# Graph layers on one core: GpSimd waits twice in a group of edges, and VectorE adds the edge bias

## The reference

```python
# layer 0
e = edge_attr @ W_edge + b_edge                 # 200000 x 128 by 128 x 256
msg = relu(x[src] + e)
agg = segment_sum(msg, dst)
h = relu(((1.0 + eps) * x + agg) @ W1 + b1) @ W2 + b2
x = layernorm(x + relu(batchnorm(h)))
# layer 1
z = x @ W                                       # 4 heads of 64
e = leaky_relu(es[src] + ed[dst]);  alpha = softmax of e over the edges of a dst
out = segment_sum(alpha * z[src], dst)
x = layernorm(x + out)
```

## Time and profile before

| | us |
|---|---|
| time before, median of 3 runs | 5048.78 (5046.24 to 5053.94) |
| the profiled execution's own time | 5007.87 |
| its span, first to last instruction | 5006.0 |
| PE busy | 3165.6 (63%) |
| POOL busy | 3022.7 (60%) |
| DVE busy | 2238.0 (45%) |
| ACT busy | 789.5 (16%) |

### The profile page before, as it was taken

How to read it: one execution, slowest core, us unless ns; L and a number is a source line. 1 busy time by engine, 2 the same in 40 slices (tenths; PEclk the granted TensorE clock), 3 DMA queues, 4 the chain that set the end, 5 groups by cost and what they waited for, 6 DMA issues and landing times.

```text
span 5006.0 us, 53159 instructions
## 1 busy us (share of the span) xinstructions
PE 3165.6 (63%) x13596; PEld 2405.9 (48%) x13597; DVE 2238.0 (45%) x4481; ACT 789.5 (16%) x1498; POOL 3022.7 (60%) x3229
## 2 busy tenths in 40 slices
PE   6878777887878778777864444444444444444455
PEld 4666655565656555555643333333333333333343
DVE  4333333333333323223355555555555555555566
ACT  2212111211222112112230000010101111111111
POOL 6666656666666556556456666666666666666654
PEclk9898888888888888888887777777777777776677
DMA  4444444444444434334254444444444444444443
GB/s 150 131 132 134 133 124 130 134 127 127 132 130 132 123 122 128 115 120 126 87 157 133 134 135 135 132 133 135 132 134 133 137 128 136 133 132 134 134 131 101
DMA packets 321267, 650.03 MB, mean 130 GB/s; under 512 B 149823, under 2 KB 170537, under 8 KB 321225
## 3 DMA queue, kind: packets, MB, share of 16 engines
q0 software_dynamic: 150272, 413.00, 29.0%
q1 hardware_dynamic: 164681, 230.37, 14.4%
q10 hardware_dynamic: 6272, 6.19, 0.4%
HBM read 636.22 MB, written 13.08 MB: 130 GB/s over the span
## 4 chain that ended last, share of the span: by engine, by line
another core or an unknown queue 36%; PE 20%; issue 19%; DVEq 12%; DVE 9%; ACT 2%; DMA 1%; SPq 0%; POOLq 0%; ACTq 0%
PE psum L1018 7%; PE psum L1029 5%; DVEq L1172 3%; PE psum L681 3%; DVEq L878 2%; DVEq L836 2%; DVE hot_t L869 2%; PE psum L1015 2%; DVE rows L1156 2%; DVEq L874 1%; DVEq L1167 1%; PE psum L1057 1%; DVE acc L1170 1%; PE psum L1038 1%
## 5 line engine op out<-in xcount | busy, mean ns | idle before, releaser
L407 POOL DMA_INDIRECT rows<-in_x,idx x1568 | 1488.4, 949 | 984.8 <-issue 453.1
L407 POOL DMA_INDIRECT rows<-z_tab,idx x1568 | 1496.7, 955 | 890.3 <-issue 466.2
L1156 DVE TENSOR_TENSOR rows<-rows,psum 128x1024 f32<-128x1024 f32 x392 | 474.7, 1220 | 1675.6 <-remote 1100.0
L1018 PE MATMUL psum<-weights,edge_room 128*128 128x256 f32 x3136 | 918.6, 417 | 48.5 <-issue 47.4
L1029 PE MATMUL psum<-rows,onehot 128*128 128x256 f32 x3136 | 853.0, 409 | 125.5 <-issue 121.9
L681 PE MATMUL psum<-rows,onehot 128*128 128x260 f32 x3136 | 911.5, 455 | 0.0
L681 PEld LDWEIGHTS psum<-rows,onehot 128*128 128x128 f32 x3136 | 721.8, 236 | 151.9
L1018 PEld LDWEIGHTS psum<-weights,edge_room 128*128 128x128 f32 x3136 | 666.3, 213 | 244.9 <-issue 90.4
L1029 PEld LDWEIGHTS psum<-rows,onehot 128*128 128x128 f32 x3136 | 624.5, 206 | 251.1 <-issue 172.7
L1102 ACT ACTIVATE rows<-rows 128x1024 f32<-128x1024 f32 x392 | 414.3, 1057 | 1952.0 <-DVE rows L1156 1410.0
L691 PE MATMUL psum<-ident,agg_sb 128*128 128x128 f32 x392 | 105.9, 363 | 657.9 <-ACT agg_sb L770 583.2
(11 more groups left out here) (155 smaller groups left out, 1672.1 us busy)
## 6 DMA issues: line engine op xcount, KB each, us to landing
dst_t<-in_dst_jp SPq DMA_DIRECT2D x197, 512.0 KB
edge_room<-in_edge_t SPq DMA_DIRECT2D x196, 512.0 KB
rows<-in_x,idx POOLq DMA_INDIRECT x1568
rows<-z_tab,idx POOLq DMA_INDIRECT x1568
z_tab<-edge_room SPq DMA_DIRECT2D x14, 455.0 KB, 6.1
idx<-in_src_idx SPq DMA_DIRECT2D x392, 4.0 KB
dst_t<-in_x_t SPq DMA_DIRECT2D x14, 448.0 KB
rows<-in_x_t SPq DMA_DIRECT2D x14, 448.0 KB, 5.0
```

Of the source, the lines that this page charges most:

```text
L407: nc.gpsimd.indirect_dma_start(rows[0:count, u, j, 0:width], None, table, bass.IndirectOffsetOnAxis(ap=idx[0:count, u, j:j + 1], axis=0)). ...
L1018: last = pe.matmul(bank[:, h * D:(h + 1) * D], edge_in[:, u, j * P:(j + 1) * P], w_edge[:, :], start=False, stop=(h == 1))
L1156: dve.tensor_tensor(half, half, psum[:, 2 * b:2 * b + 2, :].rearrange("p b (j d) -> p (b j) d", j=2), ALU.add).then_inc(added, 1)
```

## The change

In layer 0 the four bias matmuls of a group go from PE, and with them their preparation at the start. DVE adds the bias instead: two TENSOR_TENSOR per group of 128x1024 floats, `rows` plus a broadcast `b_edge`, both in SBUF, and a drain, placed once the group's 8 gathers have landed and before the first PSUM add. The PSUM add, which read `rows` and PSUM, stays.

In both layers POOL waits twice in a group, before j = 0 and before j = 4. In layer 0 the first wait is for 2g - 2, which is (g - 2, 1) done, and the second for 2g - 1, which is (g - 1, 0) done. In layer 1 the first is for the sum of group g - 3, the second for the spread of group g - 1. No DMA is added.

```diff
             def body(i, u, g):
+                close = layer == 1 and begun
                 if not first_round(i):
-                    pool.wait_ge(L.agg_ready if layer == 1 and begun else L.group_done, g - RING + 1)
+                    pool.wait_ge(L.agg_ready if close else L.group_done, g - RING + 1 + close)
...
-                gather(L, table, width, u, filled(g))
+                if close:
+                    gather(L, table, width, u, filled(g), range(J // 2))
+                    pool.wait_ge(L.edge_done, g)
+                    pool.sem_inc(passed, 1)
+                    gather(L, table, width, u, filled(g), range(J // 2, J))
...
         def single0_gathers(pool):
             def body(i, u, g):
-                pool.wait_ge(half_done, 2 * (g - RING) + 5)
+                pool.wait_ge(half_done, 2 * g - 2)
...
-                gather(layer0, t["x"], D, u, filled(g))
+                gather(layer0, t["x"], D, u, filled(g), range(J // 2))
+                pool.wait_ge(half_done, 2 * g - 1)
+                pool.sem_inc(passed, 1)
+                gather(layer0, t["x"], D, u, filled(g), range(J // 2, J))
...
-                for q in range(2):
-                    bank = banks[2 * b + q]
-                    pe.matmul(bank[:, 0:2 * D], ones_bf[:, :], bias_rhs[:, :], start=True, stop=False)
-                    for h in range(2):
-                        j = 4 * b + 2 * q + h
-                        last = pe.matmul(bank[:, h * D:(h + 1) * D], edge_in[:, u, j * P:(j + 1) * P], w_edge[:, :],
-                                         start=False, stop=(h == 1))
+                for j in range(4 * b, 4 * b + 4):
+                    last = pe.matmul(banks[j // 2][:, (j % 2) * D:(j % 2 + 1) * D], edge_in[:, u, j * P:(j + 1) * P],
+                                     w_edge[:, :], start=True, stop=True)
...
+            def add_bias(u, b):
+                half = rows[:, u, 4 * b:4 * b + 4, 0:D]
+                dve.tensor_tensor(half, half, b_edge[:, :].unsqueeze(1).to_broadcast([P, 4, D]), ALU.add)
+
...
             def body(i, u, g):
                 dve.wait_ge(layer0.rows_in[u], 16 * J * (i + 1))
+                add_bias(u, 0)
+                add_bias(u, 1)
+                dve.drain()
                 add_edges(i, u, g, 0)
```

More of the change, by code:

```diff
@@ L158, in build @@
         att = hot_t[:, :].bitcast(F32).rearrange("p (a n) -> p a n", a=2)
[L159 to L162, removed]
         plan_f = early[0:1, 24 * D:24 * D + 3 * GROUPS].rearrange("p (a n) -> p a n", a=3)
@@ L262, in build @@
         layer0, layer1 = Layer(0), Layer(1)
-        half_done, added, bias_ready = sem("half_done"), sem("added"), sem("bias_ready")
+        half_done, added = sem("half_done"), sem("added")
         a_sum = sem("a_sum")
@@ L403, in pass_loads, with gather @@
                 sp.dma_start(t["out"][lo + 3 * SUB:NODES, :], out_c[0:TAIL - 3 * SUB, 3, :]).then_inc(f_out, 16)
-        def gather(L, table, width, u, count=P):
-            for j in range(J):
+        def gather(L, table, width, u, count=P, tiles=range(J)):
+            for j in tiles:
                 nc.gpsimd.indirect_dma_start(
@@ L421, in body @@
                     pool.sem_inc(passed, 1)
-                gather(L, table, width, u, filled(g))
+                if close:
[3 more added lines that the diff above has]
+                    gather(L, table, width, u, filled(g), range(J // 2, J))
+                else:
+                    gather(L, table, width, u, filled(g))
             rounds(pool, body, begun=begun, peeled=1)
@@ L1081, in finish_last @@
                 second_product(c)
-            pe.wait_ge(bias_ready, 1)
             pe.wait_ge(const_in, 16 * WEIGHT_LOADS)
@@ L1538, in _ @@
             dve.wait_ge(edge_w_in, 48)
[L1539 to L1557, removed]
             dve.wait_ge(dst_in, 48)
```

## The result

| | us |
|---|---|
| before, median of 5 runs | 5053.94 (5046.24 to 5060.54) |
| after, median of 5 runs | 5012.31 (5009.00 to 5027.57) |
| ratio after to before | 0.992, 95% interval 0.989 to 0.995 |
| the profiled execution of after | 5014.18, its span 5012.3 |

The changed kernel is 0.8% faster (41.6 us), where 5127 and slower was forecast. The range held the time; the sign was wrong. The experiments then showed something larger: the kernel before itself takes either some 5000 to 5050 us or 4085 us, and where it takes 4085, the same change makes it 4.4% slower.

A forecast was written before the change was run, and what follows sets the result against it. POOL's path was taken as the bound: 16 gathers, then a 3.8 us stop for PE signals held while it streams. -40 + 98 - 50 + 0 + 70 = +78 on 5049 gave 5127 us, range 4960 to 5320.

The forecast's parts named there:

- Node phases, +70: 26 phases of dense PE work: POOL, one group less in hand, runs dry up to 5.0 us earlier; +70 us.
- Lock, +98: Bias adds with both operands in SBUF make POOL's gathers wait for DVE, 1.0 us a cycle; +98 us.
- Mid-cycle gap, -50: Layer 0: POOL's 1.05 us gap in the middle of half the cycles goes with the nearer waits; -50 us.
- Fewer loads, -40: PE: 34 weight loads a group, not 38, may bring held signals earlier and shorten POOL's stops; -40 us.
- Layer 1, 0: Layer 1's nearer waits leave the form and length of POOL's cycle as they were; 0 us.
- A: Rival: fewer loads and half-group waits shorten stops or space them 20 gathers apart; 4893 or 4990 us; chance 0.25.
- D: Rival: lock pairs miss the gathers, node phases cost nothing, the gap goes; 5000 to 5049 us; chance 0.12.
- B: Rival: the lock catches a gather each time and the cover on DVE goes; 5300 to 5395 us; chance 0.08.
- C: Rival: POOL stops once a group, after 8 or 12 gathers; 5290 to 5790 us; chance 0.08.

The follow-up runs named there:

- bias-on-PSUM kernel: Against the kernel before: VectorE adds the bias in place to PSUM, then adds PSUM to the rows, old waits; 5053.9 us beside 5053.4, signals held.
- the farther waits: Against before: bias on VectorE in SBUF, layer 0's POOL waiting half by half for group g - 4's sums; 4994.0 us beside 5045.9, signals held.
- the free trace of before: The kernel before, unchanged, traced again where PE's signals arrive at once (free) and not late (held); 4087.2 us beside 4087.8.
- the waits alone: Layer 0's waits changed, bias left on PE, signals held: nearer waits 4966.3 us beside 4995.7, farther half-group waits 4983.4 beside 5005.8.

## Where the 41 us came from, and why the prediction was wrong

By parts, against the trace of the bias-on-PSUM kernel, which has the old waits and the time of before:

| us, one execution each | old waits | after | difference |
|---|---|---|---|
| layer 0, POOL busy | 1459.7 | 1490.3 | +31 |
| layer 0, gaps beyond 0.31 us | 511.0 | 456.2 | -55 |
| layer 0, the regular 0.3 us between gathers | 468.7 | 468.2 | 0 |
| layer 1, from its 33rd gather | 2352.6 | 2351.3 | -1 |
| all the rest of the span | 252.7 | 246.3 | -6 |
| span | 5044.7 | 5012.3 | -32 |

The rows for layer 0 run from its 33rd gather to its last. The two executions come from different comparisons, and the executions of one kernel within one held comparison lay 28 to 52 us apart (10 of the bias-on-PSUM kernel, 13 of before), so a term of less than some 20 us is not clear of noise.

As the time of a node phase I take the start of VectorE's first operation in it (the one into `acc` at line 1186 of before in layer 0, the one into `fin_ln` in layer 1). Of the 55 us, 42 lie farther than 50 us from every phase, and 13 nearer, where I had put a cost. The longest stops are in the phases, one in each. One phase shows how such a stop can become shorter, first in the trace of before:

```profile
1785.70 1.03 PE L1018 MATMUL psum<-weights,edge_room 128*128 128x256 f32 x4
...
1794.70 0.95 POOL L407 DMA_INDIRECT rows<-in_x,idx  x1 [0.30 <-issue]
1798.59 1.22 DVE L1156 TENSOR_TENSOR rows<-rows,psum 128x1024 f32<-128x1024 f32 x1 [13.03 <-remote]
...
1816.59 0.94 POOL L407 DMA_INDIRECT rows<-in_x,idx  x1 [20.95 <-PE psum L1018]
```

and after, at the same phase:

```profile
1792.81 0.95 POOL L403 DMA_INDIRECT rows<-in_x,idx  x1 [0.31 <-issue]
1797.53 0.94 POOL L403 DMA_INDIRECT rows<-in_x,idx  x1 [3.78 <-remote]
...
1814.64 0.94 POOL L403 DMA_INDIRECT rows<-in_x,idx  x1 [11.44 <-PE psum L1020]
```

Before, the half that ends at 1786.73 is seen at 1798.59, 2.9 us after POOL ran dry at 1795.65. Only then can the node phase go on, and POOL stands through all of it, 20.95 us. After, the first of the two waits stops POOL at 1793.76, POOL restarts 3.78 us later, issues four gathers during the phase and stops again: 3.78 + 11.44 = 15.22 us. I read this as the first stop letting the signal out; no run shows that apart.

That phase is one of the three in which before stood over 20 us (63 us together, 34 at the same phases after); the bias-on-PSUM kernel has two of 19.6 and 19.7. At its other ten phases before stood 7.6 to 12.3 us (89 together), and after stood longer, 8.8 to 12.6 (109). The stop of 7.69 us in the earlier trace rows, for one, was 8.78 after:

```profile
1199.65 0.94 POOL L403 DMA_INDIRECT rows<-in_x,idx  x1 [8.78 <-PE psum L1020]
```

The longest stops of the 13 phases come to 152 us before, 161 in the bias-on-PSUM kernel and 143 after.

**Node phases, +70: the step that failed.** I priced one group less in hand as if the signals came by themselves. That is the free case, where it cost 153 us. Held, it cost nothing that can be seen: all gaps within 50 us of a phase come to 310 us before, 313 in the bias-on-PSUM kernel and 300 after in layer 0, and to 243, 247 and 254 in layer 1, about -6 in all against the bias-on-PSUM trace. (In a narrower window the sum hangs on which ordinary stops fall inside.) The reading that fits is that a held signal comes because POOL stops: being further ahead only puts the stop, and with it the signal, later. My own picture, "most held ones come out 2 to 3 us after POOL has stopped", said so; I applied it to the cycle and not to the phase.

**Lock, +98: mis-sized.** The mechanism holds (141 gathers of over 1.05 us, not 10) and cost 31 to 34 us. Of the 196 pairs of adds, 168 lengthen the gathers beside them by less than 0.2 us, as the one that starts at 1067.81 in the cycle shown (1.06 us for 0.95), and the mean of a pair is 0.19 us: 0.4 us a cycle and not the 1.0 that I took. That it can cost more is shown by 1006 ns a gather with the farther waits. This error is as large as that of the node phases; only the two together turn the sign.

**Mid-cycle gap, -50: the size right, in part by luck, and partly paid back.** Gaps of 0.6 to 2.5 us went from 64 us (bias on PSUM; 50 in the first trace) to 5. But they are of two kinds. The ones that I meant, before the first gather of a cycle's second group, were 26 in the first trace (28 us) and 31 in the bias-on-PSUM one (42 us), not one in half the cycles of 1.05 us each. The others, 14 (22 us) and 15 (22 us), stand before the second gather of a group, where POOL has no wait for `half_done`. The cycle of the earlier trace rows has one that I overlooked, right after its restart at 1051.59:

```profile
1054.41 0.95 POOL L407 DMA_INDIRECT rows<-in_x,idx  x1 [1.88 <-issue]
```

They come only in every 12th group (38, 50, 62 and so on to 194 in layer 0 of before). There all 14 such groups began after a stop and all 14 have the gap, of 1.88 us each; the two of this series that began without a stop, 14 and 26, don't. A stop isn't always needed: the bias-on-PSUM trace has two of 1.33 us without one, and the free trace of before three of 1.75 to 1.88 us, all in this series of groups too. In layer 0 after, no group of the series begins after a stop, since the stops moved to other groups, and the gap is gone. No term of mine priced that, and what the gap is stays open.

The ordinary stops, of 2.5 to 5 us, grew from 289 to 312, and those of over 5 us, the phases, fell from 157 to 139: -60 + 23 - 18 = -55. That the waits alone gain was then measured, -29 and -22 us.

**Fewer loads, -40: not seen** (+0.5 us, interval -13 to +14, in the bias-on-PSUM kernel, with its added VectorE work). Whether it helps together with half-group waits stays open: both kernels with the bias on VectorE and two waits a group (ratios 0.992 and 0.989) did better than the two with waits alone (0.994 and 0.995), though they pay the lock, but the intervals touch or overlap. The bias on VectorE in SBUF with the old waits, and layer 1's waits alone, were not had where signals are held.

**Layer 1, 0: right** where held. From the 33rd gather on, traces with the old wait ranged from 2337 to 2362 us, after took 2351.

**The rivals.** A was right in sign and wrong in mechanism: one run of 20 gathers and two of 28 in layer 0, not every second. D, "nothing that matters moves" at 5000 to 5049, is what came, for nearly its reasons; the pairs of adds did not miss the gathers, though. B and C did not show. With the terms as the held traces give them, +31 for the lock, -55 for all gaps of layer 0, -1 for layer 1 and -6 for the rest, the sum is -32 us (before rounding), by one execution of each; the medians differ by -42. Whether one starts from the profiled time or from the median moves the forecast by some 41 us and does not turn its sign.

In the free behaviour the prediction's sign and the phases' mechanism are right, but its size is not: +184 us, since nothing of the -50 and -40 is there to gain and the phases cost 153 us, not 70.

## What to carry to other kernels

In these runs a wait that makes an engine less far ahead had a price where the signals came without the engine's stop, and none that could be seen where they came after it. Before costing such a wait, ask of each late signal what let it out; if it is the stop, an earlier and shorter stop may gain. And where a trace shows signals that arrive long after their work is done, take a second trace at another time or chip before tuning for it: here the same change was worth -0.8% or +4.4%.

## What the runs showed of the hardware

- One and the same kernel took 4085 or 4996 to 5054 us, and all kernels compared in one go fell on the same side. Held, a PE signal came 10 to 12 us late where POOL had been issuing indirect DMAs (36.62 to 48.19; 1079.32 to 1089.4; 1786.73 to 1798.59), 2.9 to 3.5 us after the last of them had ended; others came 8 us late. Free, it came 0.04 us late. Both kinds of trace have gathers of 0.95 us at 1.25 us intervals.
- Where signals are held, medians of before ranged over 1.2% from one comparison to another (4996 to 5054), where free over 0.1%.
- An add of 128x1024 floats takes 1.22 us with both operands in SBUF and 1.22 to 1.23 with one in PSUM; only the first delays gathers (146 against 11).
- In every 12th group of layer 0 of before, where POOL had stopped before the group's first gather, the second gather started 1.88 us after the first had ended instead of 0.3 (14 of 14; 0 of 2 where POOL had not stopped). Layer 1 has the same, 1.85 us in 16 of 16. In the free trace of before, with no stops there, 3 of the 16 groups of this series in layer 0 have such a gap and none in layer 1.
